# Layer 0 of a two-layer network on one core: first multiply between the rounding steps of h, rounding of y behind the last multiply, first turned h group copied in two pieces

## The chip, the cores and the metric

The kernel runs on one core of a Trainium2 chip. The time is the device time of one execution in microseconds (us). An execution is driven by five instruction streams that run in their own written order and meet only at semaphores: TensorE (PE; its weight loads are shown apart as PEld), VectorE (DVE), ScalarE (ACT), GpSimd (POOL) and SyncE (SP, which only starts transfers here).

## What is computed

`x` holds 16 sequences of 256 tokens with 256 features. Two layers follow each other, and each has a mixing part and a feed-forward part. The change touches the feed-forward part of layer 0, which rounds its input, its hidden values and its weights to 4-bit floating point in blocks of 16:

```
def fp4_quant_dequant(x):                  # blocks of 16 along the last axis
    scale = jnp.max(jnp.abs(xb), axis=-1, keepdims=True) / 6.0
    xn = xb / scale
    q = _GRID[jnp.searchsorted(_MID, jnp.abs(xn))] * jnp.sign(xn) * scale
def fp4_linear(x, w):
    return einsum('bsk,nk->bsn', fp4_quant_dequant(x), fp4_quant_dequant(w))

# layer 0
x = x + tanh(g_xattn[0]) * _layernorm(x) * decayed_sum(ctx * ctx)   # decay 0.9 along the sequence
y = _layernorm(x)
h = silu(fp4_linear(y, w_gate)) * fp4_linear(y, w_up)               # 256 -> 704
x = x + tanh(g_ffn[0]) * fp4_linear(h, w_down)                      # 704 -> 256
# layer 1: attention with 16 heads, then a feed-forward part with block floating point
```

## The kernel before

**Tiling.** All 16 sequences ("batches" b) stay in on-chip memory (`xres`, `ctx`), 256 tokens as two tiles of 128 (c = 0, 1). Every engine runs a function `l0_body(b)` for b = 0 to 15; batches 4 to 11 are a hardware loop with two batches in each pass, the others are written out. After it come the attention of layer 1 and its feed-forward part, which the change doesn't touch. "Body b" below is what the engines do in the call for b; it works on several batches at once.

**What passes through one body b.** TensorE first computes gate and up of batch b (`l0_gate_up`, L475) as four units u = 0 to 3, each with 12 matmuls into one of two PSUM slots. A slot holds gate and up of one half of the columns of one token tile. Unit 2 writes into the slot of unit 0, and so waits until VectorE has multiplied unit 0 (`v_mul`, L483); unit 3 waits for unit 1 in the same way. ScalarE takes silu of each unit's gate (`l0_silu`, L839), and VectorE multiplies it with up into `h` (`l0_multiply`, L1305). After unit 3 TensorE finishes batch b-1 (`l0_hidden_out`, L526): it turns (transposes) the quantised hidden values `hq` in four groups g = 0 to 3 (`l0_turn_hidden`, L496), ScalarE copies each turned group from PSUM to `hqt` (ScalarE's own `l0_hidden_out`, L845), and `l0_down` (L514) multiplies each by the down weights. Between the second turn and the first `l0_down` it turns the quantised input of batch b+1 (`l0_turn_input`, L464), which ScalarE copies to `yth` (`l0_input_out`, L833). Last comes `l0_decayed_sum` for b+3 (L453).

**How h is rounded.** After unit 3, VectorE takes the block maxima of `h` and their reciprocals (`l0_hidden_scale`, L1314: `hscale`, `hrinv`), GpSimd scales the whole tile (`l0_hidden_scaled`, L1106: `hs`), and ScalarE makes magnitudes of it (`l0_hidden_magic`, L862: `hmag`). At the start of the next body VectorE rounds in two steps (`l0_hidden_up` L1322: `hup`; `l0_hidden_codes` L1326: `hcode`), and GpSimd puts the scale back (`l0_hidden_quantised`, L1112: `hq`). The input y of the next batch goes the same way in smaller tiles (`yscale`, `ys`, `ymag`, then `l0_y_round` L1291 with `yup` and `ycode`, then `l0_y_quantised` L1099 with `yq`).

**Other work in the body.** GpSimd also adds the mixed part into the residual of batch b+2 (`l0_x_sum`, L1088), for whose layer norm VectorE waits in `l0_y_stats` (L1272). ScalarE squares `ctx` of batch b+4 (`l0_square`, L812).

**Order by hand.** There is no scheduler: each engine's order is that of its `l0_body`. VectorE (L1337): hup, hcode, multiply 0, multiply 1, x_mix, y_round, multiply 2, x_stats, multiply 3, y_stats, hidden_scale, y_low, y_scale, add_ffn. GpSimd (L1119): hq, yq, x_sum, layer norm step, hs, ys. ScalarE's order from L878 on matters for this change, since it is not part of the diff:

```
                if prv:
                    l0_hidden_out(prv, 0)
                    l0_hidden_out(prv, 1)
...
                if b.shifted(1):
                    l0_input_out(b.shifted(1))
                if b.shifted(4):
                    l0_square(b.shifted(4))
                if prv:
                    l0_hidden_out(prv, 2)
                    l0_hidden_out(prv, 3)
```

Body 15 is another function (`l0_last_body`) on VectorE, which the diff leaves alone.

Of the kernel before, what the change touches and what calls it, by code (L numbers as in the profile page):

```python
# [16 lines left out]
P = 128  # L17
# [44 lines left out]
def upto(steps, b, name):  # L62

    return b.count(len(steps), steps.index(name) + 1)
# [81 lines left out]
def build_main(nc, load, loaded, out_v, g_xattn, g_ffn, w_gate_up, w_down, w_fc, b_fc, w_proj, b_proj, ident, decay,  # L146
# [3 lines left out]
    with ExitStack() as keep:  # L150
# [5 lines left out]
        def high(name, shape, dt):  # L156
            return right.enter_context(nc.sbuf_tensor(name, shape, dt, side="right"))
# [4 lines left out]
        def sem(name):  # L162
            return keep.enter_context(nc.semaphore(name))
# [64 lines left out]
        hqt = high("hqt", [P, 2 * C, KH0 // 2, P], F32)  # L228
# [69 lines left out]
        g_xsum, g_ys, g_yq, g_hs, g_hq = (sem(f"g_{n}") for n in ("xsum", "ys", "yq", "hs", "hq"))  # L298
        a_sq, a_xn, a_yn, a_yt = sem("a_sq"), sem("a_xnorm"), sem("a_ynorm"), sem("a_yt_high")
        a_ymag, a_hmag = sem("a_ymag"), sem("a_hmag")  # L300
        a_silu, a_ht = sem("a_silu"), sem("a_ht")
        t_r, t_yt, t_gu, t_ht, t_o = sem("t_r"), sem("t_yt"), sem("t_gu"), sem("t_ht"), sem("t_o")
        alone = sem("waits_alone")
# [20 lines left out]
        def flat(t):  # L324
            return t.rearrange("p c d -> p (c d)")
# [87 lines left out]
        def _(pe):  # L413
# [50 lines left out]
            def l0_turn_input(b):  # L464
                pe.wait_ge(g_yq, b.count(1, 1))
                if b.shifted(1):
                    pe.wait_ge(v_mix, b.shifted(1).count(1, 1))
                bank = flat(ps_r[:, :, :])
                for kc in range(KD):
                    for c in range(C):  # L470
                        ins = nc.tensor.transpose(bank[:, (kc * C + c) * P:(kc * C + c + 1) * P],
                                                  yq[:, c, kc * P:(kc + 1) * P], idf[:, :])
                ins.then_inc(t_yt, 1)
# [22 lines left out]
            def l0_turn_hidden(b, g):  # L496
                c, first_k = g // 2, (g % 2) * (KH0 // 2)
                if g == 0:
                    pe.wait_ge(g_hq, b.count(1, 1))
                    if not b.shifted(-1):  # L500
                        pe.wait_ge(a_w2, KH0 // 2)
                if g >= 2:
                    pe.wait_ge(a_ht, b.count(4, g - 1))
                elif b.shifted(-1):
                    pe.wait_ge(a_ht, b.shifted(-1).count(4, g + 3))
                bank = (ps_ta, ps_tb)[g % 2]
                for n in range(KH0 // 2):
                    k = first_k + n
                    rows = P if k < KH0 - 1 else LAST0
                    ins = nc.tensor.transpose(bank[0:rows, n * P:(n + 1) * P],  # L510
                                              hq[:, c * I0 + k * P:c * I0 + k * P + rows], idf[:, :])
                ins.then_inc(t_ht, 1)

            def l0_down(b, g):  # L514
                c, first_k = g // 2, (g % 2) * (KH0 // 2)
                pe.wait_ge(a_ht, b.count(4, g + 1))
                if g == 0 and b.shifted(-1):
                    pe.wait_ge(v_out, b.shifted(-1).count(1, 1))
                for n in range(KH0 // 2):
                    k = first_k + n  # L520
                    rows = P if k < KH0 - 1 else LAST0
                    ins = nc.tensor.matmul(ps_o[:, c, :], hqt[0:rows, g, n, :], w2t[0:rows, k, :],  # L522
                                           start=k == 0, stop=k == KH0 - 1)
                ins.then_inc(t_o, 1)

            def l0_hidden_out(b, nxt):  # L526
                l0_turn_hidden(b, 0)
                l0_turn_hidden(b, 1)
                if nxt:
                    l0_turn_input(nxt)  # L530
                l0_down(b, 0)
                l0_turn_hidden(b, 2)
                l0_down(b, 1)
                l0_turn_hidden(b, 3)
                l0_down(b, 2)
                l0_down(b, 3)
# [244 lines left out]
        def _(act):  # L781
# [63 lines left out]
            def l0_hidden_out(b, g):  # L845
                act.wait_ge(t_ht, b.count(4, g + 1))
                if b.shifted(-1):
                    act.wait_ge(t_o, b.shifted(-1).count(4, g + 1))
                bank = (ps_ta, ps_tb)[g % 2]
                if g % 2 == 0:  # L850
                    nc.scalar.copy(hqt[:, g].rearrange("p a b -> p (a b)"), bank[:, 0:3 * P]).then_inc(a_ht, 1)  # L851
                else:
                    nc.scalar.copy(hqt[0:LAST0, g, 2, :], bank[0:LAST0, 2 * P:3 * P])
                    nc.scalar.copy(hqt[:, g, 0:2].rearrange("p a b -> p (a b)"), bank[:, 0:2 * P]).then_inc(a_ht, 1)
# [197 lines left out]
        def _(pool):  # L1052
# [35 lines left out]
            def l0_x_sum(b):  # L1088
                pool.wait_ge(v_mix, b.count(1, 1))
                nc.gpsimd.tensor_tensor(tiles(xres, b), tiles(xres, b), mix[:, b.par], ALU.add).then_inc(g_xsum, 1)  # L1090
# [28 lines left out]
            def l0_body(b):  # L1119
                if not b.shifted(1):  # L1120
                    at_k_parts(first)
                if b.shifted(-1):
                    l0_hidden_quantised(b.shifted(-1))
                if not b.shifted(1):
                    at_rstd(first)
                    at_q_parts(first)
                if b.shifted(1):
                    l0_y_quantised(b.shifted(1))
                if b.shifted(2):
                    l0_x_sum(b.shifted(2))  # L1130
                    l0_ln_step(b.shifted(4), b.shifted(2))
                l0_hidden_scaled(b)
                if b.shifted(2):
                    l0_y_scaled(b.shifted(2))
# [20 lines left out]
            def at_q_parts(b):  # L1155
                qb = a_qn[:, :, :].rearrange("p c d -> p (c d)")
                pool.wait_ge(a_v_qk, upto(v_qk_steps(b), b, "norm1"))
                nc.gpsimd.tensor_tensor(a_part_cos[:, 0, :], qb, a_cos[:, :], ALU.mult).then_inc(a_g_qk, 1)
                nc.gpsimd.tensor_tensor(a_part_sin[:, 0, :], qb, a_sin[:, :], ALU.mult).then_inc(a_g_qk, 1)
# [86 lines left out]
        def _(dve):  # L1246
# [58 lines left out]
            def l0_multiply(b, u):  # L1305
                c, half = u // 2, u % 2
                dve.wait_ge(a_silu, b.count(4, u + 1))
                if u == 0 and b.shifted(-1):
                    dve.wait_ge(g_hs, b.shifted(-1).count(1, 1))
                at = c * I0 + half * HALF  # L1310
                nc.vector.tensor_tensor(h[:, at:at + HALF], sg[:, u, :], ps_gu[:, 2 * (u % 2) + 1, 0:HALF],  # L1311
                                        ALU.mult).then_inc(v_mul, 1)
# [9 lines left out]
            def l0_hidden_up(b):  # L1322
                dve.wait_ge(a_hmag, b.count(1, 1))
                nc.vector.scalar_tensor_tensor(hup[:, :], hmag[:, :], FP4_FLOOR, hs[:, :], ALU.max, ALU.add).then_inc(v_hround, 1)  # L1324

            def l0_hidden_codes(b):  # L1326
                dve.wait_ge(v_hround, upto(V_ROUND, b, "up"))
                if b.shifted(-1):
                    dve.wait_ge(g_hq, b.shifted(-1).count(1, 1))
                nc.vector.scalar_tensor_tensor(hcode[:, :], hmag[:, :], FP4_FLOOR, hup[:, :], ALU.max, ALU.subtract).then_inc(v_hround, 1)  # L1330
# [6 lines left out]
            def l0_body(b):  # L1337
                prv, nxt, nxt2 = b.shifted(-1), b.shifted(1), b.shifted(2)
                if not nxt:
                    return l0_last_body(b)  # L1340
                if prv:
                    l0_hidden_up(prv)
                    l0_hidden_codes(prv)
                l0_multiply(b, 0)
                l0_multiply(b, 1)
                if not prv:
                    w_scale(W2)
                    w_times(W2)
                if nxt2:
                    l0_x_mix(nxt2)  # L1350
                l0_y_round(nxt)
                l0_multiply(b, 2)
                if b.shifted(4):
                    l0_x_stats(b.shifted(4))
                l0_multiply(b, 3)
                if nxt2:
                    l0_y_stats(nxt2)
                l0_hidden_scale(b)
                if not prv:
                    w_up(W2)  # L1360
                    w_round(W2)
                    w_dequant(W2)
                l0_y_low(nxt)
                if nxt2:
                    l0_y_scale(nxt2)
                if prv:
                    l0_add_ffn(prv)
# [377 lines left out]
```

## Time and profile before

| | us |
|---|---|
| three timed runs | 857.71, 859.51, 860.60 (median 859.51) |
| the profiled execution, device time | 860.34 |
| its span, first to last instruction | 858.2 |

| engine | busy us | share of the span |
|---|---|---|
| TensorE matmuls | 713.5 | 83% |
| VectorE | 708.5 | 83% |
| ScalarE | 488.0 | 57% |
| GpSimd | 431.1 | 50% |

Layer 0 takes the span from about 45 to 345 us. The shares are means over three stages with different limits, so they don't say what bounds layer 0. Rows of the trace below have the start of an instruction (us from the start of the span), its duration, engine, line and operation, the tile that it writes and those that it reads, how many like it stand in the row, and in brackets the idle time just before it with what ended it. Matmuls are pipelined: the next can start before one ends, so distances between starts are what counts on TensorE. The granted clock (PEclk) is a share of TensorE's full 2.4 GHz, and 0.50 is 1.2 GHz.

### The profile page before, as it was taken

To read this page: it belongs to the slowest core of one execution; us is meant where nothing else is said; L and a number is where in the kernel's file an instruction comes from. 1 tells how busy PE (TensorE), PEld (TensorE's weight loads), DVE (VectorE), ACT (ScalarE), POOL (GpSimd) and SP (SyncE) were. 2 spreads that over 40 slices of the span, in tenths; PEclk is the share of its full clock that TensorE was granted. 3 is DMA by queue.
4 is the path that set the end of the run, shared out by engine and by line. 5 is a ranking of instruction groups with operands and counts; after the bars stand their busy time and mean duration, and the time that the engine had idled before them with its cause. 6 is when DMAs were issued, how large, how long until landed. Compare 5 with 4: busy or idle time off the path is not lost.

```text
span 858.2 us, 16571 instructions
## 1 busy us (share of the span) xinstructions
PE 713.5 (83%) x5090; PEld 517.0 (60%) x5090; DVE 708.5 (83%) x1230; ACT 488.0 (57%) x939; POOL 431.1 (50%) x331
## 2 busy tenths in 40 slices
PE   2255999999999998779999999999999775777775
PEld 1255888887888877556565555656565333444444
DVE  6867788998889887868898989898888658888885
ACT  3433545445454342337777777777778674555553
POOL 4524565555655545644444554555443526655553
PEclk8576999999999999879999999999999987888898
DMA  8800000000000000010000000000001000100011
GB/s 279 246 3 0 1 1 1 0 0 0 0 0 1 1 1 1 1 50 2 3 2 2 1 1 1 2 1 1 1 1 50 2 1 1 37 25 24 26 37 50
DMA packets 17719, 18.35 MB, mean 21 GB/s; under 512 B 1670, under 2 KB 16912, under 8 KB 17680
## 3 DMA queue, kind: packets, MB, share of 16 engines
q1 hardware_dynamic: 17084, 17.66, 6.4%
q8 instruction: 21, 0.34, 0.2%
q10 hardware_dynamic: 596, 0.20, 0.1%
q14 instruction: 18, 0.15, 0.1%
HBM read 13.39 MB, written 4.19 MB: 20 GB/s over the span
## 4 chain that ended last, share of the span: by engine, by line
PE 33%; DVE 30%; issue 16%; POOL 9%; ACT 8%; DVEq 1%; DMA 1%; POOLq 1%; ACTq 0%; SPq 0%
PE a_ps_t L561 7%; PE a_ps_m L579 6%; DVE maxima L1497 5%; PE a_ps_pv L615 4%; DVE f_ps_small L1582 4%; PE a_ps_s L600 3%; POOL hs L1110 3%; PE ps_o L522 3%; DVE hup L1324 2%; DVE f_hcode L1598 2%; DVE yup L1293 2%; POOL xres L1090 2%; DVE hscale L1318 2%; ACT hmag L866 1%; PE a_ps_pv L623 1%
## 5 line engine op out<-in xcount | busy, mean ns | idle before, releaser
L1497 DVE TENSOR_REDUCE maxima<-a_ps_m 128x2 f32<-128x512 f32 x256 | 166.3, 687 | 35.4 <-PE a_ps_m L579 34.7
L919 ACT ACTIVATE probs<-a_ps_s 128x512 f32<-128x512 f32 x256 | 149.2, 602 | 42.3 <-PE a_ps_s L600 40.1
L579 PE MATMUL a_ps_m<-stack_t 64*128 64x256 f32 x512 | 107.5, 328 | 19.9 <-DVE maxima L1497 16.7
L579 PEld LDWEIGHTS a_ps_m<-stack_t 64*128 64x128 f32 x512 | 68.3, 188 | 78.7 <-DVE maxima L1497 49.5
L600 PE MATMUL a_ps_s<-stack_t 64*128 64x256 f32 x512 | 100.0, 308 | 3.7 <-ACT probs L919 2.9
L1141 POOL TENSOR_TENSOR stack<-roped,stack 128x512 f32<-128x512 f32 x32 | 42.6, 1333 | 116.8 <-DVE stack L1487 115.3
L491 PE MATMUL ps_gu<-w1h,yth 128*128 128x352 f32 x256 | 88.6, 346 | 13.2 <-DVE h L1311 13.2
L522 PE MATMUL ps_o<-w2t,hqt 128*128 128x256 f32 (+1 forms) x384 | 97.9, 390 | 0.2 <-ACT hqt L851 0.2
L615 PE MATMUL a_ps_pv<-probs,v_aug 128*32 128x256 f32 x1024 | 83.0, 396 | 2.9 <-ACT probs L919 2.5
L910 ACT CAST stack_t<-a_ps_t 128x512 fp32r<-128x512 f32 x128 | 70.9, 588 | 24.5 <-PE a_ps_t L561 23.7
L561 PE MATMUL a_ps_t<-idf,stack 128*128 128x128 f32 x512 | 77.2, 294 | 9.0 <-POOL stack L1141 4.6
L492 PE MATMUL ps_gu<-w1l,yth 128*128 128x352 f32 x256 | 84.2, 329 | 0.0
L493 PE MATMUL ps_gu<-w1h,ytl 128*128 128x352 f32 x256 | 84.1, 328 | 0.0
L843 ACT ACTIVATE sg<-ps_gu 128x352 f32<-128x352 f32 x64 | 29.6, 462 | 84.3 <-PE ps_gu L493 84.3
L522 PEld LDWEIGHTS ps_o<-w2t,hqt 128*128 128x128 f32 (+1 forms) x384 | 66.4, 189 | 17.5 <-issue 10.6
L600 PEld LDWEIGHTS a_ps_s<-stack_t 64*128 64x128 f32 x512 | 68.5, 187 | 12.7 <-ACT probs L919 6.6
L561 PEld LDWEIGHTS a_ps_t<-idf,stack 128*128 128x128 f32 x512 | 58.8, 148 | 22.0 <-ACT stack_t L910 8.1
L1116 POOL TENSOR_TENSOR hq<-hcode,hscale 128x1408 f32<-128x1408 bf16 x16 | 41.4, 2590 | 49.5 <-DVE hcode L1330 49.5
L1190 POOL TENSOR_TENSOR f_hup<-f_h,f_hmag 128x2048 f32<-128x2048 f32 x16 | 58.2, 3640 | 10.5 <-DVE f_hcode L1598 9.5
L491 PEld LDWEIGHTS ps_gu<-w1h,yth 128*128 128x128 f32 x256 | 49.5, 193 | 18.6 <-DVE h L1311 17.5
L980 ACT ACTIVATE f_h<-f_ps_fc 128x512 f32<-128x512 f32 x64 | 36.1, 597 | 36.0 <-POOL f_hup L1190 33.7
L703 PE MATMUL f_ps_h<-idb,f_hcode 128*128 128x128 bf16 x256 | 25.9, 261 | 33.6 <-DVE f_hcode L1598 33.5
(176 smaller groups left out, 1613.3 us busy)
## 6 DMA issues: line engine op xcount, KB each, us to landing
xres<-in_x SPq DMA_DIRECT2D x16, 256.0 KB, 3.2
ctx<-in_ctx SPq DMA_DIRECT2D x16, 256.0 KB, 3.8
out_x<-f_y SPq DMA_DIRECT2D x16, 256.0 KB, 2.1
w1a_raw<-in_w_gate_up SPq DMA_DIRECT2D x1, 1024.0 KB, 6.2
w_raw<-in_w_fc SPq DMA_DIRECT2D x1, 1024.0 KB, 5.7
w_raw<-in_w_proj SPq DMA_DIRECT2D x1, 1024.0 KB, 5.0
w_raw<-in_w_down SPq DMA_DIRECT2D x1, 704.0 KB, 9.3
stack_t<-neg_max_t SPq DMA_DIRECT2D x32, 8.0 KB
```

The lines of the kernel that those rows point to most:

```text
L491: nc.tensor.matmul(into, yth[:, kc, c, :], w1h[:, kc, cols], start=kc == 0, stop=False)
L492: nc.tensor.matmul(into, yth[:, kc, c, :], w1l[:, kc, cols], start=False, stop=False)
L493: ins = nc.tensor.matmul(into, ytl[:, kc, c, :], w1h[:, kc, cols], start=False, stop=kc == KD - 1)
L522: ins = nc.tensor.matmul(ps_o[:, c, :], hqt[0:rows, g, n, :], w2t[0:rows, k, :], start=k == 0, stop=k == KH0 - 1)
L561: ins = nc.tensor.transpose(a_ps_t[:, g % 2, (n * C + c) * P:(n * C + c + 1) * P], a_stack[:, b.par, which, c, 2 * pair:2 * pair + 2, :].r ...
L579: ins = nc.tensor.matmul(a_ps_m[:, half, n, :], a_stack_t[b.par][rows, 0, pair, c * P:(c + 1) * P], a_stack_t[b.par][rows, 1, pair, :], st ...
L600: ins = nc.tensor.matmul(a_ps_s[:, half, n, :], a_stack_t[b.par][rows, 1, pair, kc * P:(kc + 1) * P], a_stack_t[b.par][rows, 0, pair, :], ...
L615: ins = nc.tensor.matmul(a_ps_pv[32 * n:32 * n + 32, quad % 2, 0:T], a_v_aug[:, b.par, kc, 4 * quad + n, :], a_probs[:, (2 * g + n % 2) % ...
L910: nc.scalar.copy(a_stack_t[b.par][:, g % 2, pair:pair + 2, :].rearrange("p a t -> p (a t)"), a_ps_t[:, g % 2, :]).then_inc(a_t, 1)
L919: nc.scalar.activation(a_probs[:, u % 8], a_ps_s[:, u % 2], ACT.Exp).then_inc(a_exp, 1)
L1190: nc.gpsimd.tensor_tensor(f_blocks(f_hup[:, :]), f_blocks(f_h[:, b.par]), f_spread(f_hmag[:, b.par], F_NBH), ALU.add).then_inc(f_g_hup, 1)
L1497: nc.vector.tensor_reduce(a_maxima[:, b.par, c, 4 * quad + half:4 * quad + half + 3:2], a_ps_m[:, half], X, ALU.max).then_inc(a_v_max, 1)
```

## The change

VectorE multiplies unit 0 between the two rounding steps of h (it stood behind both), and rounds y behind multiply 3 (it stood ahead of multiply 2). GpSimd adds into the residual ahead of scaling y back. TensorE turns the next batch's input behind the second `l0_down`, and no longer ahead of the first. ScalarE copies the first turned group of h in two pieces, the first with a semaphore of its own, so that the first down matmul can start on it. ScalarE's order of calls stays as it was.

```
@@ PE @@
             def l0_down(b, g):
                 c, first_k = g // 2, (g % 2) * (KH0 // 2)
-                pe.wait_ge(a_ht, b.count(4, g + 1))
+                if g:
+                    pe.wait_ge(a_ht, b.count(4, g + 1))
+                else:
+                    pe.wait_ge(a_ht_first, b.count(1, 1))
                 if g == 0 and b.shifted(-1):
                     pe.wait_ge(v_out, b.shifted(-1).count(1, 1))
                 for n in range(KH0 // 2):
+                    if g == 0 and n == 1:
+                        pe.wait_ge(a_ht, b.count(4, 1))
                     k = first_k + n
...
             def l0_hidden_out(b, nxt):
                 l0_turn_hidden(b, 0)
                 l0_turn_hidden(b, 1)
-                if nxt:
-                    l0_turn_input(nxt)
                 l0_down(b, 0)
                 l0_turn_hidden(b, 2)
                 l0_down(b, 1)
+                if nxt:
+                    l0_turn_input(nxt)
                 l0_turn_hidden(b, 3)
                 l0_down(b, 2)
                 l0_down(b, 3)
@@ ACT @@
                 bank = (ps_ta, ps_tb)[g % 2]
-                if g % 2 == 0:
+                if g == 0:
+                    nc.scalar.copy(hqt[:, 0, 0], bank[:, 0:P]).then_inc(a_ht_first, 1)
+                    nc.scalar.copy(hqt[:, 0, 1:3].rearrange("p a b -> p (a b)"), bank[:, P:3 * P]).then_inc(a_ht, 1)
+                elif g % 2 == 0:
                     nc.scalar.copy(hqt[:, g].rearrange("p a b -> p (a b)"), bank[:, 0:3 * P]).then_inc(a_ht, 1)
@@ POOL @@
+                if b.shifted(2):
+                    l0_x_sum(b.shifted(2))
                 if b.shifted(1):
                     l0_y_quantised(b.shifted(1))
                 if b.shifted(2):
-                    l0_x_sum(b.shifted(2))
                     l0_ln_step(b.shifted(4), b.shifted(2))
@@ DVE @@
                 if prv:
                     l0_hidden_up(prv)
+                l0_multiply(b, 0)
+                if prv:
                     l0_hidden_codes(prv)
-                l0_multiply(b, 0)
                 l0_multiply(b, 1)
                 if not prv:
                     w_scale(W2)
                     w_times(W2)
                 if nxt2:
                     l0_x_mix(nxt2)
-                l0_y_round(nxt)
                 l0_multiply(b, 2)
                 if b.shifted(4):
                     l0_x_stats(b.shifted(4))
                 l0_multiply(b, 3)
+                l0_y_round(nxt)
                 if nxt2:
                     l0_y_stats(nxt2)
                 l0_hidden_scale(b)
```

## Rows read from the trace of the kernel before

**Rows 1.** Busy time in stretches, body 7 (us, busy and count, PEclk, DMA, GB/s)

```profile
184.89:202.69 17.80, 17.11 (x96) 14.60 (x95) 15.92 (x25) 8.75 (x18) 10.07 (x10) 1.00 0.00 0
```

**Rows 2.** The instructions in order of time, VectorE, body 7

```profile
184.89 1.63 DVE L1324 SCALAR_TENSOR_TENSOR hup<-hmag,hs 128x1408 f32<-128x1408 bf16 x1 [0.46 <-ACT hmag L866]
...
188.09 0.99 DVE L1311 TENSOR_TENSOR h<-sg,ps_gu 128x352 f32<-128x352 f32 x2
...
189.66 1.82 DVE L1293 SCALAR_TENSOR_TENSOR yup<-ymag,ys 128x512 f32<-128x512 bf16 x1
...
195.91 1.62 DVE L1318 TENSOR_REDUCE hscale<-h 128x88 f32<-128x1408 f32 x1
```

**Rows 3.** The same of GpSimd, body 7

```profile
188.33 2.60 POOL L1116 TENSOR_TENSOR hq<-hcode,hscale 128x1408 f32<-128x1408 bf16 x1 [3.33 <-DVE hcode L1330]
...
192.36 1.06 POOL L1103 TENSOR_TENSOR yq<-ycode,yscale 128x512 f32<-128x512 bf16 x1 [1.43 <-DVE ycode L1297]
...
193.38 1.27 POOL L1090 TENSOR_TENSOR xres<-xres,mix 128x512 f32 x1
```

**Rows 4.** The same of VectorE, body 2: yup with GpSimd idle

```profile
101.88 0.68 DVE L1293 SCALAR_TENSOR_TENSOR yup<-ymag,ys 128x512 f32<-128x512 bf16 x1
```

**Rows 5.** The same of TensorE, body 7 and the start of body 8

```profile
183.84 0.51 PE L491 MATMUL ps_gu<-w1h,yth 128*128 128x352 f32 x1
...
188.66 0.43 PE L491 MATMUL ps_gu<-w1h,yth 128*128 128x352 f32 x1 [0.63 <-DVE h L1311]
...
192.61 0.49 PE L510 MATMUL ps_ta<-idf,hq 128*128 128x128 f32 x3
...
193.48 0.66 PE L471 MATMUL ps_r<-idf,yq 128*128 128x128 f32 x4
...
193.97 1.46 PE L522 MATMUL ps_o<-w2t,hqt 128*128 128x256 f32 x6
...
195.60 1.66 PE L522 MATMUL ps_o<-w2t,hqt 128*128 128x256 f32 x6
...
197.18 0.55 PE L510 MATMUL ps_tb<-idf,hq 128*128 128x128 f32 x3
...
197.57 2.95 PE L522 MATMUL ps_o<-w2t,hqt 128*128 128x256 f32 x12
...
201.66 0.51 PE L491 MATMUL ps_gu<-w1h,yth 128*128 128x352 f32 x1
```

**Rows 6.** The same of TensorE: decayed sums that close bodies 1, 2 and 11

```profile
94.84 0.70 PE L460 MATMUL ps_r<-sq,dec 128*128 128x256 f32 x2
...
111.59 0.70 PE L460 MATMUL ps_r<-sq,dec 128*128 128x256 f32 x2
...
272.19 0.70 PE L460 MATMUL ps_r<-sq,dec 128*128 128x256 f32 x2
```

**Rows 7.** The same of ScalarE, body 7

```profile
192.80 0.46 ACT L843 ACTIVATE sg<-ps_gu 128x352 f32<-128x352 f32 x1 [1.45 <-PE ps_gu L493]
...
193.52 0.27 ACT L853 COPY hqt<-ps_tb 64x128 f32<-64x128 f32 x1
...
194.17 0.58 ACT L837 CAST yth<-ps_r 128x512 fp32r<-128x512 f32 x1
194.65 0.63 ACT L816 ACTIVATE sq<-ctx 128x512 f32 x1
...
195.80 0.48 ACT L851 COPY hqt<-ps_ta 128x384 f32<-128x384 f32 x1 [0.51 <-PE ps_ta L510]
```

**Rows 8.** The same of TensorE, body 15, where no input is turned

```profile
338.50 1.56 PE L522 MATMUL ps_o<-w2t,hqt 128*128 128x256 f32 x6 [0.19 <-ACT hqt L851]
```

**Rows 9.** The same of VectorE, body 0

```profile
60.56 0.75 DVE L1250 BATCH_NORM_STATS2 stats<-xres 128x6 f32<-128x256 f32 x2 [0.68 <-POOL xres L1090]
```

**Rows 10.** TensorE behind the longest idles, bodies 1 and 14; then its busy time and clock

```profile
81.68 0.48 PE L491 MATMUL ps_gu<-w1h,yth 128*128 128x352 f32 x1 [1.84 <-DVE h L1311]
...
313.21 0.43 PE L491 MATMUL ps_gu<-w1h,yth 128*128 128x352 f32 x1 [1.73 <-DVE h L1311]
...
82.00:84.00 2.00, 2.00 (x8) 0.50 0.00 0
```

More of the change, by code:

```diff
@@ L300, in build_main @@
         a_ymag, a_hmag = sem("a_ymag"), sem("a_hmag")
+        a_ht_first = sem("a_first_hidden_part")
         a_silu, a_ht = sem("a_silu"), sem("a_ht")
@@ L515, in l0_down @@
                 c, first_k = g // 2, (g % 2) * (KH0 // 2)
-                pe.wait_ge(a_ht, b.count(4, g + 1))
+                if g:
+                    pe.wait_ge(a_ht, b.count(4, g + 1))
+                else:
+                    pe.wait_ge(a_ht_first, b.count(1, 1))
                 if g == 0 and b.shifted(-1):
@@ L519, in l0_down @@
                 for n in range(KH0 // 2):
+                    if g == 0 and n == 1:
+                        pe.wait_ge(a_ht, b.count(4, 1))
                     k = first_k + n
@@ L528, in l0_hidden_out @@
                 l0_turn_hidden(b, 1)
-                if nxt:
-                    l0_turn_input(nxt)
                 l0_down(b, 0)
@@ L533, in l0_hidden_out @@
                 l0_down(b, 1)
+                if nxt:
+                    l0_turn_input(nxt)
                 l0_turn_hidden(b, 3)
@@ L849, in l0_hidden_out @@
                 bank = (ps_ta, ps_tb)[g % 2]
-                if g % 2 == 0:
+                if g == 0:
+                    nc.scalar.copy(hqt[:, 0, 0], bank[:, 0:P]).then_inc(a_ht_first, 1)
+                    nc.scalar.copy(hqt[:, 0, 1:3].rearrange("p a b -> p (a b)"), bank[:, P:3 * P]).then_inc(a_ht, 1)
+                elif g % 2 == 0:
                     nc.scalar.copy(hqt[:, g].rearrange("p a b -> p (a b)"), bank[:, 0:3 * P]).then_inc(a_ht, 1)
@@ L1126, in l0_body @@
                     at_q_parts(first)
+                if b.shifted(2):
+                    l0_x_sum(b.shifted(2))
                 if b.shifted(1):
@@ L1129, in l0_body @@
                 if b.shifted(2):
-                    l0_x_sum(b.shifted(2))
                     l0_ln_step(b.shifted(4), b.shifted(2))
@@ L1342, in l0_body @@
                     l0_hidden_up(prv)
+                l0_multiply(b, 0)
+                if prv:
                     l0_hidden_codes(prv)
-                l0_multiply(b, 0)
                 l0_multiply(b, 1)
@@ L1350, in l0_body @@
                     l0_x_mix(nxt2)
-                l0_y_round(nxt)
                 l0_multiply(b, 2)
@@ L1355, in l0_body @@
                 l0_multiply(b, 3)
+                l0_y_round(nxt)
                 if nxt2:
```

## The prediction

> **What bounds the kernel now.** The diff touches layer 0 only, so I read there: first the busy times of a body, then the chain of waits through one, then each engine in order of time. In body 7 TensorE is busy for 17.11 of 17.80 us, VectorE for 15.92, ScalarE for 8.75 and GpSimd for 10.07, at a granted clock of 1.00 [rows 1]. Two engines are nearly full, so the order of waits decides. Two loops run side by side.
>
> The first is TensorE's own work. Body 2 runs without a wait that counts: its closing decayed sum begins 16.75 us after that of body 1 [rows 6]. That is TensorE's floor. Bodies 2 to 11 together take 272.19 - 94.84 = 177.35 us, 17.74 each [rows 6], so about 1 us per body is waiting. Body 7 shows where: 0.63 us ahead of unit 2, which waits for multiply 0, and a short wait for yq ahead of turning the input (about 0.2: two turns of three begin at 192.61, and the input only at 193.48) [rows 5].
>
> The second loop goes through VectorE and sets those waits. hup begins at 184.89; its twin hcode stands ahead of multiply 0, which starts at 188.09 [rows 2], and TensorE resumes at 188.66 [rows 5]. After mix comes yup, which takes 1.82 us [rows 2] although the same instruction takes 0.68 when GpSimd is idle [rows 4]. It ends at 191.48, about 0.55 after GpSimd's hq (188.33 + 2.60) [rows 3]: it was held up behind it. Then GpSimd runs yq and only behind it the residual sum, until 194.65 [rows 3]. VectorE needs that sum for its statistics, so hscale begins at 195.91 [rows 2], and from hscale to the next hup (202.69) it is 6.78 us [rows 1, 2]. TensorE's floor is only 1 us below this loop.
>
> **The VectorE and GpSimd edits remove the second loop.** No instruction is added; two are moved on each engine. Count from S, the start of unit 0 on TensorE, and Y, the start of the first turn of h. In body 7 they lie 192.61 - 183.84 = 8.77 apart [rows 5]; without the 0.63 of idle and its draining and refilling some 7.9 remain.
> - Multiply 0 goes behind hup. It can't start before silu of unit 0, some 2.8 after S, as silu of unit 3 begins 0.19 after its matmuls and takes 0.46 [rows 5, 7]. It ends near S + 3.3, ahead of the end of units 0 and 1 near S + 4.0. The 0.63 of idle goes.
> - hcode is thereby held back to about S + 3.25 to 4.9. hq follows with 0.15 and 2.60 [rows 3] and ends near S + 7.6, ahead of Y at 7.9. The cover is 0.2 to 0.3 us; if it is gone, TensorE waits ahead of the first turn.
> - yup and ycode stand behind multiply 3, when hq is over: 0.68 instead of 1.82, a gain of 1.1 on VectorE. The residual sum runs straight behind hq, until S + 8.9, before multiply 3 ends near Y + 1.2 = S + 9.1.
> - yq now ends near Y + 1.2 + 1.4 + 0.15 + 1.06 = Y + 3.8. The turned input, needed at Y in the old place, is now needed behind two turns and two down groups.
> - hscale begins near Y + 1.2 + 1.4 + 1.0 (statistics, 194.90 to 195.91 as now) = Y + 3.6, and the next hup 6.78 later, Y + 10.4. On its own this loop would allow a body of about 16.5 us. It no longer binds.
>
> **The TensorE edit brings a new wait.** The input is turned behind the second down group. I call that start X. From Y it is two turns, the first down group and a turn (193.97 to 195.60, 1.63), and the second down group (195.60 to 197.18, 1.58) [rows 5]: X = Y + 4.1 with the small wait below, after yq at Y + 3.8. So yq costs nothing.
>
> But ScalarE's order is not changed. There, the copy of group 2 stands behind the cast of the turned input and the square. Today the input is turned so early that both are done by the time that group 2 is turned: ScalarE even idles 0.51 ahead of that copy [rows 7]. Now the cast can't start until the input is turned. It starts 0.69 after the turn does (193.48 to 194.17) [rows 5, 7]. The square follows 0.48 later [rows 7]. The copy follows that by 0.53 (its 0.63 less the 0.10 by which neighbours overlap) and takes 0.48 [rows 7]. TensorE resumes some 0.05 behind a copy, so at X + 0.69 + 0.48 + 0.53 + 0.48 + 0.05 = X + 2.23. TensorE itself is ready at X + 0.49 + 0.39 (four transposes, then three) = X + 0.88 [rows 5]. The new idle is 1.35 us in each body. What is queued behind it is the rest of TensorE's body: down groups 2 and 3, the decayed sum, and gate and up of the next batch. There is no other wait to absorb it, since the slack in TensorE's queue is what the first edits have just used up.
>
> **The split copy.** Without the turned input between them, the first down group follows the turns at once. In body 15, where it is like this already, TensorE waits 0.19 for the whole copy [rows 8]. At full clock: silu of unit 3 begins at Y + 0.19, the copy some 0.36 later, and a piece of 128 columns takes about 0.27, like the copy of 64 x 128 [rows 7]; TensorE could start near Y + 0.86 and has been ready since about Y + 0.65. Wait: 0.2 us. The whole copy would make that 0.4. The second piece lands while the first matmul runs. One more ScalarE instruction (0.16 to 0.27) lies beside idle ScalarE time.
>
> **The sum.** New body: 16.75 + 0.20 + 1.35 = 18.30, against 17.74 on average: +0.56 in each of the ten bodies 2 to 11, +5.6. Bounds for the two waits together: 1.2 (copy and square overlap more than now) to 1.8 (full durations, one behind the other), so 17.95 to 18.55 and +2.1 to +8.1. I take 18.30, since its spacings are those of rows.
> - Body 0: hscale is freed of the 0.68 of waiting for the residual sum [rows 9], which now runs earlier: -0.7.
> - Body 1: multiply 0 comes a little earlier (idle 1.84 to about 1.6), and the two new waits come in, 1.3 in sum. The half clock behind that idle [rows 10] costs some 1.6 (twelve matmuls at 0.29 instead of 0.16) and may fall away. So +1.3 or -0.3; middle +0.5.
> - Bodies 12 to 14: no square, so a wait of 0.8 in place of 1.35; body 13 waits for hup again, body 14 gives its shorter idle back at hq. About 0, within 0.7.
> - Body 15 and all behind it have their old order, and the whole delay passes to the end of the span.
>
> Sum: +5.6 - 0.7 + 0.5 = +5.4. The profiled execution took 860.34, so 865.8; the median of the runs lies 0.8 below it, so 865.0.
>
> **The rivals.**
> - *The copy's place doesn't matter, and the kernel is faster.* All that the first edits free would be kept: a body of 16.95, ten times -0.79, and -0.5 from the start, which gives 851. For it: ScalarE is idle half the time. Against it: each of its calls is in line behind the one before, and the copy's place is in the code. It decides at a new wait of 0.8 us: below that the body is shorter than 17.74. Chance 8%.
> - *Break-even.* The wait is there but is 0.6 to 1.1, since ScalarE takes cast and square quicker than I add them up, or bodies 0, 1 and 12 to 14 give more: 860. Chance 12%.
> - *A later link joins.* hq misses Y, or yq misses X (covers of 0.2 to 0.3 each), by some 0.3 in each body: 868 to 870. Chance 8%.
> - *The clock falls.* TensorE ran at half clock behind an idle of 1.84 us and at full clock behind one of 1.73 [rows 10]. An idle of 1.35 is shorter than both, but comes in each body with smaller ones around it. Each fall costs 1.6 us: with one in every second body 874, with one in each 881. Chance 10%. The Trainium skill, "TensorE: Matmul & The Clock Gate", section "A second HAM failure mode: psum-queue depth-cycling", says that frequent short idles between groups of matmuls are enough to make the clock go up and down. By that rule this rival would be the forecast; the trace speaks against it so far, with an idle of 0.63 and a clock of 1.00 in body 7 [rows 1, 5].
> - *The forecast.* Chance 62%.
>
> **How the numbers follow.** A measurement of this kernel can tell a change of about 0.3% from none: faster is below 856.9, slower above 862.1. The range 860 to 871 holds the forecast, the late link and most of break-even, and leaves out the faster rival and the falling clock. Faster: 8%. Same: break-even and the low end of the forecast, 15%. Slower: 77%.
>
> **What would show it.** In the changed kernel, a body should take 18.3 us from one decayed sum to the next; unit 2 should wait for nothing; the down group behind the fourth turn should wait 1.3 to 1.4 us for ScalarE's copy of group 2, and the first down group 0.2; yup should take 0.7; and ScalarE should run cast, square and copy without a gap. The prediction is wrong if TensorE is found without that wait, if the idle ahead of unit 2 is still there, or if the granted clock falls below 1.00 between 100 and 290 us.

## The result and the profile after

The changed kernel is slower. Its median is 866.85 us (864.32 to 870.41, six runs) against 860.06 (857.10 to 861.08, six runs) of the kernel before. The ratio is 1.0088, with a 95% interval of 1.0059 to 1.0117. The forecast was 865.0, slower, in a range of 860 to 871.

The instructions of TensorE in order of time, body 7 of the changed kernel and the start of body 8 (these answer to rows 5 and 6; L528 is the down matmul, L472 the turn of the input, L511 that of h, L461 the decayed sum):

```profile
187.24 0.70 PE L461 MATMUL ps_r<-sq,dec 128*128 128x256 f32 x2
...
196.32 0.49 PE L511 MATMUL ps_ta<-idf,hq 128*128 128x128 f32 x3
196.64 0.49 PE L511 MATMUL ps_tb<-idf,hq 128*128 128x128 f32 x3
197.19 1.56 PE L528 MATMUL ps_o<-w2t,hqt 128*128 128x256 f32 x6
198.59 0.49 PE L511 MATMUL ps_ta<-idf,hq 128*128 128x128 f32 x3
198.91 1.66 PE L528 MATMUL ps_o<-w2t,hqt 128*128 128x256 f32 x6
200.50 0.66 PE L472 MATMUL ps_r<-idf,yq 128*128 128x128 f32 x4
200.99 0.49 PE L511 MATMUL ps_tb<-idf,hq 128*128 128x128 f32 x3
202.73 3.05 PE L528 MATMUL ps_o<-w2t,hqt 128*128 128x256 f32 x12 [1.25 <-ACT hqt L860]
205.71 0.70 PE L461 MATMUL ps_r<-sq,dec 128*128 128x256 f32 x2
```

No idle stands ahead of unit 2 any more. In its place, 1.25 us of idle stands ahead of down groups 2 and 3, and it ends with ScalarE's copy of group 2. A body takes 18.47 us here and 18.64 every second time; body 7 of before takes 17.82 (182.63 to 200.45). The same stretch on ScalarE shows why (it answers to rows 7):

```profile
201.19 0.59 ACT L843 CAST yth<-ps_r 128x512 fp32r<-128x512 f32 x1 [3.37 <-PE ps_r L472]
201.68 0.64 ACT L822 ACTIVATE sq<-ctx 128x512 f32 x1
202.21 0.47 ACT L860 COPY hqt<-ps_ta 128x384 f32<-128x384 f32 x1
```

ScalarE stands idle for 3.37 us, and through the last 2.1 of them group 2 lies turned in PSUM (from 199.08 on), since the next call in ScalarE's order is the cast of an input that isn't turned yet. Then cast, square and copy run without a gap.

The other loop has come free, as VectorE and GpSimd show (rows 2 and 3):

```profile
191.25 0.52 DVE L1321 TENSOR_TENSOR h<-sg,ps_gu 128x352 f32<-128x352 f32 x1 [1.48 <-ACT sg L849]
...
197.01 0.52 DVE L1321 TENSOR_TENSOR h<-sg,ps_gu 128x352 f32<-128x352 f32 x1 [0.41 <-ACT sg L849]
197.45 0.68 DVE L1303 SCALAR_TENSOR_TENSOR yup<-ymag,ys 128x512 f32<-128x512 bf16 x1
198.17 0.69 DVE L1307 SCALAR_TENSOR_TENSOR ycode<-ymag,yup 128x512 bf16<-128x512 bf16 x1
...
199.78 1.62 DVE L1328 TENSOR_REDUCE hscale<-h 128x88 f32<-128x1408 f32 x1
...
206.62 1.66 DVE L1334 SCALAR_TENSOR_TENSOR hup<-hmag,hs 128x1408 f32<-128x1408 bf16 x1
```

```profile
193.47 2.59 POOL L1125 TENSOR_TENSOR hq<-hcode,hscale 128x1408 f32<-128x1408 bf16 x1 [5.21 <-DVE hcode L1340]
196.03 1.27 POOL L1099 TENSOR_TENSOR xres<-xres,mix 128x512 f32 x1
199.02 1.05 POOL L1112 TENSOR_TENSOR yq<-ycode,yscale 128x512 f32<-128x512 bf16 x1 [1.72 <-DVE ycode L1307]
```

hup now starts early enough that VectorE idles 1.48 us behind it until silu of unit 0 is there. Busy time in the stretch from 96 to 275 us, before and then after (columns as in rows 1):

```profile
96.00:275.00 179.00, 172.49 (x951) 147.90 (x951) 157.62 (x251) 87.69 (x181) 101.77 (x91) 1.00 0.00 0
```

```profile
96.00:275.00 179.00, 166.74 (x919) 142.70 (x918) 135.15 (x243) 81.08 (x182) 96.72 (x86) 1.00 0.00 0
```

VectorE's busy time falls by 22 us, but the stretch also holds fewer bodies (9.7 instead of 10.1). Body by body it is 14.05 us in body 7 (187.24 to 205.71) instead of 15.92: 1.14 less in yup, and 0.8 less in the small TENSOR_SCALAR that writes yscale. TensorE does less work in the same time. VectorE stopped being a bound, and the time it gave back went into a queue on ScalarE, the engine with the least to do in this stretch.

### The profile page after: what moved, and what is told of

Read it like the earlier page. It is cut to its first block, busy times and chain, and to the rows that moved or that the text cites. A ratio compares the mean times of both kernels' runs of the same rounds, so it can differ in the third digit from the quotient of the medians.

```text
span 864.0 us, 16572 instructions
## 1 busy us (share of the span) xinstructions
PE 708.3 (82%) x5075; PEld 513.5 (59%) x5090; DVE 686.0 (79%) x1230; ACT 486.8 (56%) x955; POOL 430.7 (50%) x331
## 2 busy tenths in 40 slices
DMA packets 17719, 18.35 MB, mean 21 GB/s; under 512 B 1670, under 2 KB 16912, under 8 KB 17680
## 4 chain that ended last, share of the span: by engine, by line
PE 48%; DVE 22%; issue 13%; ACT 8%; POOL 4%; DMA 3%; DVEq 1%; SPq 1%; POOLq 1%; ACTq 0%
PE ps_o L528 8%; PE a_ps_t L567 7%; PE a_ps_m L585 6%; DVE maxima L1508 5%; PE a_ps_pv L621 4%; DVE f_ps_small L1593 4%; PE ps_gu L492 4%; PE ps_gu L494 4%; PE ps_gu L493 4%; PE a_ps_s L606 3%; DMA ctx<-in_ctx 2%; DVE f_hcode L1609 2%; PE a_ps_pv L629 1%; ACT probs L928 1%; ACT stack_t L919 1%
## 5 line engine op out<-in xcount | busy, mean ns | idle before, releaser
L585 PE MATMUL a_ps_m<-stack_t 64*128 64x256 f32 x512 | 107.8, 328 | 20.1 <-DVE maxima L1508 17.0
L528 PE MATMUL ps_o<-w2t,hqt 128*128 128x256 f32 (+1 forms) x384 | 100.6, 396 | 17.2 <-ACT hqt L860 15.9
L528 PEld LDWEIGHTS ps_o<-w2t,hqt 128*128 128x128 f32 (+1 forms) x384 | 66.2, 189 | 41.8 <-ACT hqt L860 19.6
L1321 DVE TENSOR_TENSOR h<-sg,ps_gu 128x352 f32<-128x352 f32 x64 | 33.2, 519 | 47.0 <-ACT sg L849 47.0
```

Of the source, the lines that this page charges most:

```text
L585: ins = nc.tensor.matmul(a_ps_m[:, half, n, :], a_stack_t[b.par][rows, 0, pair, c * P:(c + 1) * P], a_stack_t[b.par][rows, 1, pair, :], st ...
```

## The experiments

Eleven kernels were run beside the kernel before. "Body" is the mean distance between decayed sums on TensorE over bodies 2 to 11, read in each trace. The kernel before was timed again beside each group of kernels, with medians of 860.1 (changed kernel), 861.9 (e1 to e4), 862.4 (e5, e6, e8, e9) and 860.4 (e10, e11, e1 once more); each ratio is to the one beside.

| kernel | body, us | time, us | ratio to before, interval |
|---|---|---|---|
| before | 17.74 | 860.1 | 1 |
| changed kernel | 18.54 | 866.85 | 1.0088 (1.0059 to 1.0117) |
| e1, copy of group 2 ahead of cast and square | 17.29 | 851.96 | 0.9903 (0.9874 to 0.9932) |
| e1 once more | 17.29 | 852.64 | 0.9910 (0.9877 to 0.9943) |
| e2, only the square behind that copy | 18.02 | 862.62 | 1.0013 (0.9990 to 1.0036) |
| e3, first group copied whole | 18.76 | 868.44 | 1.0089 (1.0056 to 1.0122) |
| e8, e1 with the first group copied whole | 17.51 | 855.87 | 0.9924 (0.9895 to 0.9954) |
| e4, before with multiply 0 moved | 18.39 | 869.63 | 1.0104 (1.0066 to 1.0143) |
| e6, before with the input turned late | 18.76 | 871.18 | 1.0132 (1.0086 to 1.0178) |
| e11, before with the residual sum first | 17.90 | 860.89 | 1.0020 (0.9998 to 1.0042) |
| e5, e1 with the residual sum behind yq | 19.18 | 880.37 | 1.0230 (1.0187 to 1.0272) |
| e10, e1 with y rounded early | 18.16 | 865.21 | 1.0042 (1.0020 to 1.0064) |
| e9, changed kernel with the input turned early | 22.18 | 915.11 | 1.0594 (1.0523 to 1.0665) |

### Is it the copy's place? A full dose and a half one

```
 # e1, ScalarE's l0_body
                 if prv:
                     l0_hidden_out(prv, 0)
                     l0_hidden_out(prv, 1)
...
+                if prv:
+                    l0_hidden_out(prv, 2)
                 if b.shifted(1):
                     l0_input_out(b.shifted(1))
                 if b.shifted(4):
                     l0_square(b.shifted(4))
                 if prv:
-                    l0_hidden_out(prv, 2)
                     l0_hidden_out(prv, 3)
```

> The changed kernel with ScalarE's copy of turned group 2 moved ahead of the cast of the turned input and of the square; nothing else. Theory (the copy's place in ScalarE's order causes TensorE's new wait of 1.25 us): that wait goes, a body takes 17.2 to 17.3 us instead of 18.5, and the time falls by 13 to 15 us to 851 to 854, below the kernel before. Rival (the body is set by something else, such as the later rounding of y or the later hcode, and the wait only shows it): the idle moves to another place, the time stays within 2 us of 867.

The time was 851.96 us, and 852.64 when run once more. TensorE in the same place of e1, body 8:

```profile
210.62 0.66 PE L472 MATMUL ps_r<-idf,yq 128*128 128x128 f32 x4
211.11 0.49 PE L511 MATMUL ps_tb<-idf,hq 128*128 128x128 f32 x3
211.44 3.21 PE L528 MATMUL ps_o<-w2t,hqt 128*128 128x256 f32 x12
```

One call moved on ScalarE turns a loss of 0.9% into a gain of 0.9% to 1.0%. The wait went, and no idle of its size came back elsewhere. Down groups 2 and 3 are not quite free, though: they take 3.13 us from start to start (211.44 to 214.57) where the changed kernel has 2.98. In e1 ScalarE's copies of group 3 stand behind cast and square and end at 212.84, 1.40 us after group 2 begins, about when TensorE needs them; that this makes the 0.15 fits the times and was not tested.

```
 # e2, ScalarE's l0_body
                 if b.shifted(1):
                     l0_input_out(b.shifted(1))
+                if prv:
+                    l0_hidden_out(prv, 2)
                 if b.shifted(4):
                     l0_square(b.shifted(4))
                 if prv:
-                    l0_hidden_out(prv, 2)
                     l0_hidden_out(prv, 3)
```

> The changed kernel with only the square moved behind the copy of group 2; the cast stays ahead of it. A half dose. Theory: the wait of 1.25 us shortens by the square's 0.53 to about 0.7, a body takes 18.0 us, the time falls by 5 to 6 us to about 861. Rival (the square lies beside other work): no change, 867.

Measured: 862.62, body 18.02, and this wait:

```profile
198.35 3.05 PE L528 MATMUL ps_o<-w2t,hqt 128*128 128x256 f32 x12 [0.73 <-ACT hqt L860]
```

It shortened by 0.52, the spacing of one square, and the body by the same. What stands ahead of the copy counts one for one. This version runs level with the kernel before, so the point of decision lies at a wait of about 0.7 (0.8 in the prediction).

### The split copy

The edits undo the split: one wait for `a_ht` ahead of `l0_down`, one copy of 384 columns. e3 does it to the changed kernel, e8 to e1.

> The changed kernel with the first turned group copied in one piece again. Theory: the first down group starts 0.2 us later in each body (0.87 against 1.08 us behind the first turn), and since TensorE sets the body, all of it counts: +3 us, 870. Rival (the wait for group 2 behind it absorbs it, because ScalarE's cast is what counts): no change, 867.

> The kernel of e1 with the first turned group copied in one piece. Theory: TensorE sets the body, so the 0.2 us of e3 counts here as well: a body takes 17.4 us, +2 to +3 us on e1, 854 to 855. Rival (the loop through hup sets e1's body): as e1, 852.

The body grew by 0.22 in both. The wait ahead of the first down group is 0.27 to 0.42 with the whole copy, and at most 0.18 with the pieces. The medians moved by +1.6 (e3) and +3.2 or +3.9 (e8 against the two runs of e1), and e3's ratio to before is that of the changed kernel (1.0089 and 1.0088). Single comparisons of this kernel hardly resolve such a step; the body length does. The split was worth what it was costed at.

### One edit at a time on the kernel before

```
 # e4, VectorE's l0_body
                 if prv:
                     l0_hidden_up(prv)
+                l0_multiply(b, 0)
+                if prv:
                     l0_hidden_codes(prv)
-                l0_multiply(b, 0)
```

> The kernel before with one edit: multiply 0 between the two rounding steps. Theory (two loops; the one through hup, hcode, hq, yup, residual sum and hscale sets the body): TensorE's idle ahead of unit 2 goes, but hcode comes 0.43 us later and yup still waits for hq, so a body takes 18.3 to 18.4 instead of 17.9: +4 to +6 us, about 865. Rival (the idle of 0.63 ahead of unit 2 is the loss itself): -6 us, 854.

It was 869.63, body 18.39. That body is as expected, the time 4 to 5 us above it. The expectation had set the body against 17.9 instead of 17.74 and 860 instead of the 861.9 beside it, and had left out bodies 0 and 1, which are 1.1 us longer (the sum that closes body 1 starts at 95.98 instead of 94.84): 861.9 + 6.6 + 1.1 is 869.6. The idle ahead of unit 2 went, and another took its place, ahead of turning the input:

```profile
199.16 0.66 PE L471 MATMUL ps_r<-idf,yq 128*128 128x128 f32 x4 [1.47 <-POOL yq L1103]
```

The idle of 0.63 that one sees first in the trace of before was no loss of its own. It was the place where the loop through hup was felt. Filling it lengthens the loop by the multiply: body 7 takes 18.35 instead of 17.82, and the multiply 0.52.

```
 # e6, TensorE's l0_hidden_out
                 l0_turn_hidden(b, 1)
-                if nxt:
-                    l0_turn_input(nxt)
                 l0_down(b, 0)
                 l0_turn_hidden(b, 2)
                 l0_down(b, 1)
+                if nxt:
+                    l0_turn_input(nxt)
```

> The kernel before with TensorE's edit alone: the input turned behind the second down group. Theory (cast and square ahead of the copy of group 2 cost TensorE 1.25 us wherever the input is turned late, and the first down group then waits for the whole copy, 0.4): a body takes 18.7 us as in e3, 867 to 869. Rival (the loss comes from VectorE's later steps, not from this move): no slower than 861.

871.18, with the body of e3 to the hundredth, and both waits as in e3:

```profile
218.03 1.56 PE L522 MATMUL ps_o<-w2t,hqt 128*128 128x256 f32 x6 [0.42 <-ACT hqt L851]
...
223.57 2.84 PE L522 MATMUL ps_o<-w2t,hqt 128*128 128x256 f32 x11 [1.25 <-ACT hqt L851]
```

So this one move makes the whole loss of bodies 2 to 11: TensorE's order alone gives 18.76 with a whole copy, and with it in place VectorE's and GpSimd's edits don't change that length. They do bring something outside these bodies: the first matmul of the attention starts at 349.72 in before, 358.18 in e3 and 359.97 in e6.

### Were the other moves needed?

e9 is the changed kernel with `l0_turn_input` back ahead of the first `l0_down`.

> The changed kernel with the input turned in its old place, ahead of the first down group. Theory: yq is ready only 3.9 us behind the first turn of h, TensorE is ready at 0.65 and waits 3.2 us in each body, a body takes 20.1 us, about 885. Rival (TensorE's move was not needed, and the old place avoids the wait for ScalarE at no price): about 850 to 855.

The direction held, but it came out 30 us slower than expected: 915.11. The wait for yq is there, and something more. First TensorE in body 7 of e9; then its busy times in the 3.5 us behind that wait and in the long stretch (columns as in rows 1, where the granted clock is 0.53 and 0.89):

```profile
221.53 1.01 PE L472 MATMUL ps_r<-idf,yq 128*128 128x128 f32 x4 [3.00 <-POOL yq L1112]
```

```profile
221.50:225.00 3.50, 3.47 (x11) 2.83 (x12) 2.79 (x4) 1.12 (x2) 2.59 (x5) 0.53 0.00 0
96.00:275.00 179.00, 154.73 (x759) 130.70 (x758) 115.20 (x204) 71.07 (x154) 81.43 (x73) 0.89 0.00 1
```

An idle of 3.0 us in each body halves TensorE's clock behind it, from 2.4 to 1.2 GHz. Each body then takes 21.5 to 22.9 us where 20.1 had been counted. The expectation left the clock out, and with it about 2 us per body.

e5 moves GpSimd's `l0_x_sum` back behind `l0_y_quantised` in the kernel of e1.

> The kernel of e1 with GpSimd's residual sum back behind yq. Theory (the loop through hscale and hup binds as soon as VectorE's statistics wait for the sum): the sum ends 5.0 us behind the first turn of h instead of before it, hscale and hup come 2.7 us later, TensorE idles some 1.8 us ahead of unit 2, a body takes 19.0 us, and the time is about 870. Rival (with TensorE's wait for ScalarE gone, the place of the sum on GpSimd costs nothing): 852, as e1.

880.37, body 19.18. The statistics wait for the sum as costed:

```profile
207.97 0.75 DVE L1260 BATCH_NORM_STATS2 stats<-xres 128x6 f32 x2 [2.69 <-POOL xres L1100]
```

The 10 us beyond the expectation are mine: a body longer by 1.9 makes 19 us over ten bodies, and the others pay as well, which I had not added: 4.0 up to the sum that closes body 1 (97.55 instead of 93.52), and 5.1 behind body 11. Nor does TensorE's wait stand where I had put it. Ahead of unit 2 it is 0.34 in body 7; the larger one stands ahead of the decayed sum, which waits for VectorE:

```profile
212.26 0.67 PE L461 MATMUL ps_r<-sq,dec 128*128 128x256 f32 x2 [0.99 <-DVE ytl L1311]
```

### Two misses: the residual sum alone, and y rounded early

e11 is the kernel before with GpSimd's edit alone. e10 is e1 with `l0_y_round` back ahead of multiply 2.

> The kernel before with GpSimd's edit alone: the residual sum ahead of yq. Theory (the loop through hup, hq, yup, yq, residual sum and hscale set the body of before at 17.9): the sum now ends while ycode runs, the statistics start 0.85 us earlier, yq itself is not later, a body takes 17.0 to 17.1 us, about 852, with one of the diff's edits. Rival (yq behind the sum makes TensorE wait for the turned input, up to 1.3 us): 18 us or more, 862 or slower.

> The kernel of e1 with the rounding of y back ahead of multiply 2. Theory: yup is held up behind hq again (1.8 us or more instead of 0.7), hscale comes about 0.5 us later behind the first turn, but hup still arrives before silu of unit 0 plus its own length, so TensorE keeps a body of 17.2 to 17.3 us, 852 to 853. Rival (the 1.1 us of yup sits on the chain that sets the body): a body of 18.3, 863.

> The kernel of e1 once more, beside the two others on the same chip. Theory and rival: 852, a body of 17.2 to 17.4 us. It tells e11 from e1: if both have the same body within 0.1 us, the other edits of the diff bring nothing that the residual sum doesn't.

Both expectations failed. e11 gained nothing (860.89 where 852 was expected), and e10 lost 13 us on e1 (865.21 where 852 was expected). The same thing happens in both. e11, VectorE and then GpSimd:

```profile
209.37 0.95 DVE L1294 SCALAR_TENSOR_TENSOR yup<-ymag,ys 128x512 f32<-128x512 bf16 x1
210.35 1.66 DVE L1298 SCALAR_TENSOR_TENSOR ycode<-ymag,yup 128x512 bf16<-128x512 bf16 x1
```

```profile
207.18 2.59 POOL L1116 TENSOR_TENSOR hq<-hcode,hscale 128x1408 f32<-128x1408 bf16 x1 [3.40 <-DVE hcode L1331]
209.73 1.74 POOL L1090 TENSOR_TENSOR xres<-xres,mix 128x512 f32 x1
```

In the kernel before, yup is held up behind hq and ycode then runs alone, for GpSimd has nothing to do until ycode is there. With the sum straight behind hq, ycode is held up too: 1.66 instead of 0.69, and the sum itself takes 1.74 instead of 1.27. yq ends 1 us later, and TensorE waits 1.13 for it. e10 shows the same with yup at 2.29 and ycode at 1.65 (body 7), and VectorE idles 0.46 there ahead of hup, waiting for hmag: the loop through hup sets the body again, as the rival of that expectation has it. I had moved the sum in my head without asking what it would now run beside. The Trainium skill, "GPSIMD Engine Reference", section "8. Key points", says that GpSimd shares its interfaces to the on-chip memory with VectorE and contends with those of its instructions that run in a 2-port mode or have two inputs there. These traces agree: yup and ycode have two such inputs and are held up, while mix, with one input in PSUM, keeps its 0.74 beside hq. Two inputs are not needed, though. This one has a single input and, beside hs (180.77 to 183.36 on GpSimd), takes 1.10 in the kernel before, where its shortest is 0.18:

```profile
182.29 1.10 DVE L1279 TENSOR_SCALAR yscale<-yscale 128x32 f32<-128x32 f32 x1
```

Whether it runs in a 2-port mode no trace shows.

The two edits therefore belong together. The early sum is what frees hscale (e5 without it: 19.18), and the late rounding is what keeps the early sum from colliding (e10 without it: 18.16). Only with both is it 17.29.

## Why the prediction was right, and where it was off

- **Two loops a microsecond apart.** Shown. With TensorE's new wait taken away, e1 reaches a body of 17.29. With the edits put singly on the kernel before (e4, e11), the body stays at 17.9 or above, and VectorE still waits for hmag ahead of hup (0.46 and 0.34), so the loop through hup is closed there.
- **Multiply 0 between the rounding steps.** The 0.63 went in the changed kernel and in e4. hq ends at 196.06 and TensorE needs it at 196.32: the cover of 0.2 to 0.3 held, and it is used up now.
- **yup.** 0.68, as forecast. yq ends 3.75 behind the first turn (forecast 3.8).
- **The new wait.** X + 2.23 was worked out; 202.73 - 200.50 is 2.23. e1 and e2 show that it is this wait which costs, and in proportion.
- **The split copy.** First down group 0.87 behind the first turn (forecast 0.86), worth 0.22 per body.
- **The term that was mis-sized.** The body is 18.54, not 18.30, so bodies 2 to 11 cost +8.1 and not +5.6. The floor of 16.75 came from body 2 of before, and there TensorE has these rows:

```profile
104.58 0.60 PE L471 MATMUL ps_r<-idf,yq 128*128 128x128 f32 x4
105.02 1.56 PE L522 MATMUL ps_o<-w2t,hqt 128*128 128x256 f32 x6
106.41 0.49 PE L510 MATMUL ps_ta<-idf,hq 128*128 128x128 f32 x3
...
108.71 2.95 PE L522 MATMUL ps_o<-w2t,hqt 128*128 128x256 f32 x12
```

  Set against them, body 7 of the changed kernel (18.47) is longer by 1.72, where 1.55 had been added. The new wait makes 1.36 of it and the one ahead of the first down group 0.23, both nearly as forecast. Two things were left out: down groups 2 and 3, started behind a wait, take 2.98 from start to start instead of 2.88 (108.71 to 111.59 [rows 6]), and turning the input takes 0.49 instead of 0.44. The first down group adds nothing (1.40 and 1.39). The last 0.07 of the 0.24 come from every second body: 4, 6, 8 and 10, the first of each pass of the hardware loop, are 0.17 longer than the others, and this shows ahead of the second turn and of the first down group. Body 2, written out, has nothing of that kind. Why a pass starts slower no trace shows.
- **The other bodies.** Bodies 0 and 1 were forecast together at -0.2; the sum that closes body 1 starts at 94.52 instead of 94.84 [rows 6]: -0.3. The clock fall behind the 1.84 us of idle [rows 10] didn't come. The idle is 0.99 now, but that its length decided is not shown: see the last section. Bodies 12 to 15, forecast at 0, added 0.2.
- **Behind layer 0.** Up to the attention the changed kernel is 7.9 us behind: the same matmul starts there at 360.22 before and 368.15 after. Yet the profiled spans differ by 5.8 only. The rest was given back in stages that the diff doesn't touch, most of it in the last: VectorE is 8.0 us behind the kernel before at 732 us of the span and 6.6 behind at 792. The forecast had +5.4 for all of layer 0, where 7.9 were measured. That the median came out within 1.9 us of 865.0 is therefore in part luck: a main term 2.5 too small, and 2.1 given back where nothing had been forecast.
- **The rivals.** "The copy's place doesn't matter" fell with e1. "Break-even" had the wait at 0.6 to 1.1; it was 1.25, and e2 with 0.73 shows that the time would have been level there. "The clock falls" didn't occur in the changed kernel: with 1.25 us of idle and smaller ones in every body the granted clock is 1.00 from 96 to 275 us. What the Trainium skill, "TensorE: Matmul & The Clock Gate", section "A second HAM failure mode: psum-queue depth-cycling", says of frequent short idles is not borne out at this size; e9 shows the clock falling in each body at idles of 3.0 us. "A later link joins" didn't occur, with covers of 0.26 left at hq and 0.43 at yq.

What stays open is the order of e4 and e3. e4 has a shorter body (18.39 against 18.76), and in the profiled executions it is ahead, with a span of 864.6 against 865.3; yet its median is 1.2 us higher. With four and five runs and spreads of 4.3 and 3.5 us, that can't be told from chance.

## What to carry to other kernels

When a step is moved on one engine, go through the written order of every engine that takes its result. What stands behind the consumer there is moved as well, and here that cost 1.25 us per body and turned a gain of 8 to 10 us into a loss of 7. An idle in the trace can be only the place where a loop is felt: fill it, and the loop gets longer (e4). And before moving work on GpSimd, look at what VectorE would run beside it in the new place, since edits which pay together can be worth nothing one by one (e10, e11).

## What the hardware showed that I had not expected

- VectorE and GpSimd hold each other up instruction by instruction. yup alone takes 0.68; begun while hq runs it takes 0.95 (e11), 1.82 (before) or 2.29 (e4, e10), and in each of these it ends 0.55 after hq does. ycode takes 0.69 alone and 1.65 to 1.66 with GpSimd's sum in line behind hq, and the sum itself grows from 1.27 to 1.74.
- TensorE's clock fell behind an idle of 1.84 us and not behind one of 1.73 [rows 10], but the line doesn't lie between them. In body 1 of e6 the idle in the same place is 2.06, and the clock stays at 1.00 behind it (in e5 it is 1.98, with the same outcome):

```profile
81.64 0.43 PE L491 MATMUL ps_gu<-w1h,yth 128*128 128x352 f32 x1 [2.06 <-DVE h L1311]
```

```profile
82.00:84.00 2.00, 2.00 (x15) 2.00 (x14) 1.94 (x3) 0.16 (x2) 1.84 (x1) 1.00 0.00 0
```

  All thirteen profiled executions have an idle of 1.92 or 1.93 us ahead of unit 3 of body 15; in before it is longer than both idles of rows 10. Within 2 us of its end the clock has fallen to 0.50 in five of them (before, changed kernel, e9, e10, e11) and stays at 1.00 in the other eight. So at about 1.8 to 2.1 us the length of the idle doesn't decide, and a cost for it can only be forecast as a chance. At the ends it was clear: idles of 2.8 to 3.15 us in each body of e9 brought a fall each time (mean clock 0.89), and 1.25 us in each body of the changed kernel or 1.3 to 1.65 in each of e4 never did (mean clock 1.00 from 96 to 275 us in both).
- The spread of the changed kernel's runs goes with the clock granted over the whole run: 864.3 us at a mean of 0.956, 866.1 at 0.939, 870.4 at 0.927. The runs of e1 don't show it (851.2 at 0.936, 851.7 at 0.932, 856.5 at 0.934). In the last stage the profiled run of before has 0.87 and that of after 0.91:

```profile
680.00:858.00 178.00, 129.22 (x915) 78.23 (x914) 139.25 (x260) 100.72 (x166) 89.43 (x48) 0.87 0.07 24
```

```profile
680.00:864.00 184.00, 128.97 (x961) 79.46 (x972) 144.16 (x270) 105.90 (x175) 92.54 (x49) 0.91 0.07 24
```

That goes with the 2.1 us which the changed kernel made up behind layer 0, without being proof of it. No run varied the clock of that stage alone. In a kernel like this, a few microseconds of a median can be the clock's, and the distance between two rows in the stage that was changed is the better measure.
